# Inner chunks in pairs with row-paired products, and token products spread over a turn, in a vision layer on one core

## The reference

```
h = patches(x) @ W + b                                   # 768 -> 192
h = h + attention(layernorm(h))                          # 12 heads of 16, rope, causal,
                                                         # weights erf(score / 4) + 1, divided by their sum
f = layernorm(h)
shared = silu(f @ s1) * (f @ s3) @ s2                    # 192 -> 768 -> 192, every token
top2 of softmax(f @ Wr) over 8 experts, at most 3920 tokens an expert, by weight
routed[e] = silu(f_e @ w1[e]) * (f_e @ w3[e]) @ w2[e]    # times the token's weight, added to its row
out = h + shared + routed
```

## Time and profile before

| | us |
|---|---|
| median of 3 runs | 3695.66 (3693.1 to 3698.46) |
| profiled execution | 3705.55 |
| its span, first to last instruction | 3703.7 |
| attention stage, about | 0 to 1755 |
| routing stage, about | 1755 to 1909 |
| shared units, about | 1913 to 2378 |
| last shared unit and start of the routed ones | 2378 to 2405 |
| routed units, about | 2405 to 3685 |

### The profile page before, as it was taken

How to read it: one execution, slowest core, us unless ns; L and a number is a source line. 1 busy time by engine, 2 the same in 40 slices (tenths; PEclk the granted TensorE clock), 3 DMA queues, 4 the chain that set the end, 5 groups by cost and what they waited for, 6 DMA issues and landing times. The chain is left out here.

```text
span 3703.7 us, 76882 instructions
## 1 busy us (share of the span) xinstructions
PE 3398.9 (92%) x26932; PEld 2416.6 (65%) x26932; DVE 2472.7 (67%) x4826; ACT 1570.9 (42%) x3198; POOL 1432.8 (39%) x1302
## 2 busy tenths in 40 slices
PE   5999999999999999998249999899999999999997
PEld 4777777777777777776226566666666666666665
DVE  5988898888888989897645555554454444445443
ACT  2444444444444445443014444344444444444443
POOL 0222232222222222232215553136556555555664
PEclk8787788877877888775569999999999999999999
DMA  3332333223323332222012222213232232323222
GB/s 95 71 69 61 75 82 69 68 70 80 69 62 75 82 69 73 65 53 56 35 50 63 66 72 71 83 31 66 38 61 42 59 63 39 60 38 61 41 40 31
DMA packets 330541, 227.05 MB, mean 61 GB/s; under 512 B 209103, under 2 KB 309551, under 8 KB 326159
## 3 DMA queue, kind: packets, MB, share of 16 engines
q1 hardware_dynamic: 259536, 163.94, 17.4%
q0 software_dynamic: 57472, 48.46, 8.8%
q10 hardware_dynamic: 13262, 10.65, 0.8%
HBM read 107.75 MB, written 67.85 MB: 47 GB/s over the span
## 5 line engine op out<-in xcount | busy, mean ns | idle before, releaser
L1272 DVE SCALAR_TENSOR_TENSOR ffn_hidden<-ffn_up,ffn_silu 128x490 f32<-128x490 f32 (+2 forms) x534 | 358.1, 672 | 802.3 <-ACT ffn_silu L1255 731.4
L699 POOL TENSOR_TENSOR weights<-weights,x_pair 128x400 f32<-128x400 f32 x384 | 397.2, 1034 | 918.1 <-DVE weights L563 733.7
L1255 ACT ACTIVATE ffn_silu<-ffn_gate 128x490 f32<-128x490 f32 (+2 forms) x534 | 310.9, 583 | 702.4 <-PE ffn_up L1223 635.7
L615 DVE RECIPROCAL recip<-x_product 128x200 f32<-128x200 f32 x384 | 534.4, 1392 | 0.0
L1240 PE MATMUL ffn_out<-ffn_w_hi,ffn_hidden_hi 128*126 128x192 f16 (+2 forms) x2124 | 522.5, 246 | 0.0
L1242 PE MATMUL ffn_out<-ffn_w_hi,ffn_hidden_lo 128*126 128x192 f16 (+2 forms) x2124 | 522.4, 246 | 0.0
L1241 PE MATMUL ffn_out<-ffn_w_lo,ffn_hidden_hi 128*126 128x192 f16 (+2 forms) x2124 | 522.3, 246 | 0.0
L1428 POOL DMA_INDIRECT out_rows<-done,kept x256 | 425.9, 1664 | 150.4 <-issue 98.1
L1418 POOL DMA_INDIRECT tokens<-dram_x,ids x256 | 279.6, 1092 | 397.5 <-issue 258.9
L750 PE MATMUL bank<-w_qkv,normed_t 96*128 96x192 f32 (+1 forms) x1024 | 399.8, 555 | 19.1 <-ACT normed_t L413 19.1
L1265 DVE TENSOR_TENSOR ffn_hidden_lo<-ffn_hidden,ffn_hidden_hi 128x490 f16<-128x490 f32 (+2 forms) x534 | 355.4, 666 | 8.4
(11 more groups left out here) (181 smaller groups left out, 7429.8 us busy)
## 6 DMA issues: line engine op xcount, KB each, us to landing
patches<-in_patches SPq DMA_DIRECT2D x32, 1176.0 KB, 5.1
ffn_raw<-in_w SPq DMA_DIRECT2D x18, 768.0 KB
dram_x_t<-x_t SPq DMA_DIRECT2D x32, 392.0 KB, 3.1
x_t<-dram_x_t SPq DMA_DIRECT2D x24, 512.0 KB, 5.2
base<-dram_h SPq DMA_DIRECT2D x24, 384.0 KB
out_rows<-sums ACTq DMA_DIRECT2D x24, 384.0 KB
v_held<-v SPq DMA_DIRECT2D x64, 102.0 KB, 2.3
dram_h<-h SPq DMA_DIRECT2D x32, 192.0 KB
```

Of the source, the lines that this page charges most:

```text
L615: nc.vector.reciprocal(recip[:, n % 2], x_product[:, n % 2]).then_inc(inverted, 1)
L699: nc.gpsimd.tensor_tensor(weights[:, n % 4], weights[:, n % 4], x_pair[:, n % 4, ::-1], ALU.mult)\
L1255: nc.scalar.activation(T.silu[:, m % 2, 0:n], T.gate[m % 2][:, 0:n], ACT.Silu, scale=1.0 / (TOKEN_SCALE * WEIGHT_SCALE)).then_inc(T.silued, 1)
L1272: nc.vector.scalar_tensor_tensor(T.hidden[:, m % 2, 0:n], T.up[m % 2][:, 0:n], HIDDEN_SCALE / (TOKEN_SCALE * WEIGHT_SCALE), T.silu[:, m % ...
```

## The change

Two things are done. In the attention stage the token product of images u+2 stands at steps 0, 1, 7 and 8 of a turn, a tile at each, instead of 7, 8 and twice 11; the positions of the bank tuples shift with it, and ACT copies the halves at steps 1 and 8 instead of 8 and 11. In the feed-forward stage the inner chunks are made two at a time. The "lo x far" product takes 64 rows of the array instead of 128: gate's in rows 0 to 63, up's in rows 64 to 127 against a second copy of the far tokens' hi part (`far_again`), both at the end of a pair of chunks. After each pair of chunks comes a third of `tensor_out`, the transposes come after the first pair, and the split of the next unit's tokens moves on ACT and DVE to chunk m = 3, into a second set of buffers. ACT gets one more activation a unit. The clearing of the low weight halves goes away, since all 128 rows are now computed.

```diff
 LN1T, QK, VV, YT, PROJ, X2T, ROUTE, TOK = (
-    (0, 1), (2, 3, 4, 5), (6, 9), (7, 8), (10, 11), (13, 14), (16,), (12, 15))
+    (1, 2), (3, 4, 5, 6), (7, 10), (8, 9), (11, 12), (14, 15), (17,), (0, 13))
...
-                    if n in (8, 11) and has_tokens:
-                        k = n // 11
+                    if n in (1, 8) and has_tokens:
+                        k = n // 8
...
-                    if n in (7, 8) and has_tokens:
-                        if n == 7:
+                    if n in (0, 1, 7, 8) and has_tokens:
+                        if n == 0:
...
-                        tokens(n - 7)
+                        tokens(n if n < 2 else n - 5)
...
-                    if n == 11 and has_tokens:
-                        tokens(2)
-                        tokens(3)
...
-            for w_lo in T.w_lo:
-                for lo in w_lo[0:2]:
-                    n += 1
-                    nc.gpsimd.memset(lo[D - 128:128, INNER:2 * INNER], 0.0).then_inc(enlarged, 1)
-                    pool.wait_ge(enlarged, n)
...
+def tokens_hi(nc, T, slot, near, far, n):
+
+    nc.scalar.activation(T.near_hi[slot][:, 0:n], near, ACT.Copy, scale=TOKEN_SCALE).then_inc(T.tokens_hi, 1)
+
+    nc.scalar.activation(T.far_again[slot][D - 128:128, 0:n], far[D - 128:128], ACT.Copy, scale=TOKEN_SCALE)
+    nc.scalar.activation(T.far[slot][:, 0:n], far, ACT.Copy, scale=TOKEN_SCALE).then_inc(T.tokens_hi, 1)
...
-            nc.tensor.matmul(out, hi[:, far], far_both, start=False, stop=False)
-            last = nc.tensor.matmul(out, lo[:, far], far_both, start=False, stop=True)
-        last.then_inc(T.gated, 1)
+            nc.tensor.matmul(out, hi[:, beyond], far, start=False, stop=False)
+    for m in (2 * pair, 2 * pair + 1):
+        beyond = slice(INNER + m * 128, INNER + (m + 1) * 128)
+        nc.tensor.matmul(T.gate[m % 2][:, 0:n], T.w_lo[ws][0][top, beyond], far[top], start=False, stop=True)\
+          .then_inc(T.gated, 1)
+        nc.tensor.matmul(T.up[m % 2][:, 0:n], T.w_lo[ws][1][low, beyond], far_again[low], start=False, stop=True)\
+          .then_inc(T.gated, 1)
...
+def tensor_out(nc, pe, T, g, slot, ws, tiles, third):
...
+    share = len(tiles) * MI // 3
+    for k in range(third * share, (third + 1) * share):
+        t, m = divmod(k, MI)
...
         if m:
             hi(m - 1)
+        if m == 3:
+            split()
     hi(MI - 1)
...
-                tensor_unit(nc, pe, T, g, ws, XU)
-                if not closing(e, i, 7):
-                    turn(v + 1, half + i % 2, 1 - i % 2)
-                if opening(e, i):
-                    tensor_out(nc, pe, T, g - 1, 0, 0, SHORT)
-                else:
-                    tensor_out(nc, pe, T, g - 1, i % 2, 1 - ws if i == 0 else ws, ROUTED)
+                for part in range(3):
+                    tensor_pair(nc, pe, T, g, 1 - i % 2, ws, XU, part)
+                    if part == 0 and not closing(e, i, 7):
+                        turn(v + 1, half + i % 2, 1 - i % 2)
+                    if opening(e, i):
+                        tensor_out(nc, pe, T, g - 1, 0, 0, SHORT, part)
+                    else:
+                        tensor_out(nc, pe, T, g - 1, i % 2, 1 - ws if i == 0 else ws, ROUTED, part)
```

136 lines of the change are left out of this document (71 added, 65 removed).

## The result

The changed kernel takes **3724.1 us** (median of 4 runs, 3722.0 to 3728.7) against 3694.4 us for the kernel before (4 runs, 3690.7 to 3698.5): ratio 1.0073, 95% interval 1.0049 to 1.0096. It is slower, and lies outside the forecast range of 3560 to 3690.

The account below looks back on a forecast made before the run. It took DVE's work plus PE's low clock to bound attention, and PE, with POOL close behind, the routed units. Terms -91 - 16 - 3 + 19 + 6 + 1 = -84 gave 3621.5 profiled, 3612 us median; range 3560 to 3690.

Parts of the forecast that it names:

- What bounds the kernel, attention: Attention turns: DVE's list is the floor, 47.3 us; the 49.0 and 56.0 us turns differ by PE's clock.
- The attention part: Attention: moving token tiles from step 11 lets step 3's q/k products run at full clock; turns 49.4 us, -91 us.
- rival A: Attention: the clock stays low at step 3, turns 51.5 us, attention gives only -30, total 3672 us; chance 0.16.
- That costs little, because PE waits there for DVE's masks anyway: Attention, step 0: the token tile starts at half clock, 4.3 us instead of 2.15, at little cost.
- Half products: Feed-forward: 64-row halves run at once; a pair of chunks takes 3.92 us instead of 4.13, 0.62 less a routed unit.
- Rival D: Feed-forward: the halves don't run at once, 267 pairs lose 0.2 us each, total 3680 us; chance 0.05.
- Shared units: Feed-forward, 24 shared units: each gets 0.65 us shorter, -16 us.
- Routed units: 64 routed units: gathered rows due 8.5 us earlier, no unit shorter than 19.6 us; -3 us (-38 to +38).
- B's sign: Routed units: no wait for gathered rows before L217 and units of 19.0 us; chance 0.12.
- C: Routed units: gathered rows become the bound, slower; the likelier case, with attention at -30, is 3727 us; chance 0.11.
- Units i = 1: Routed units i = 1: put waits behind ACT's weights, DVE's lower weights hold the second pair; +19 us (0 to +40).
- Last shared unit: Last shared unit: transposes of gathered rows stand behind the first pair, so everything waits for them; 31.9 us against 25.9, +6.

Follow-up runs that it names:

- e14: e12 with token tiles 0 and 1 both at step 2 instead of steps 1 and 2; ratio 0.9515 to the kernel before, attention 1515.0 us.
- e5: The kernel before with PE's attention loop written out, so no jumps back; ratio 0.9882, attention 1607.1 us.
- e6: The changed kernel with PE's attention loop written out; ratio 0.9828 to the kernel before, attention 1613.6 us.
- e8: e6 with token tiles 0 and 1 at steps 1 and 2 instead of 0 and 1; ratio 0.9677, attention 1547.8 us.
- e1: The kernel before with only the attention part of the change; ratio 1.0052, attention 1687.5 us.
- e2: The changed kernel with the attention part taken back, only the feed-forward part left; ratio 0.9986.
- e10: e8 with the transposes behind the second pair of chunks, in the last shared unit behind the third; ratio 0.9636, routed units 1281.0 us.
- e11: e10 with ACT's put ahead of the next expert's upper weights in unit 1 of an expert; ratio 0.9681, routed units 1294.3 us.
- e13: e12 with put ahead of the upper weights and DVE's lower weights at the end of unit 6 instead of unit 1; ratio 0.9559, routed units 1251.2 us.
- e12: e10 with PE's feed-forward loops written out as well; ratio 0.9639, routed units 1267.7 us.

## Why the prediction was wrong

- **What bounds the kernel, attention.** Half right. DVE's list is the floor: 47.3 us were worked out, and 47.8 is what `e14` reached. But "what differs is PE's clock" was read from two rows with different clocks and different lengths, and the long turn of the two was also the one with the loop's jump. The view of waits has the 35.1 us of PE for issue, 13 times, and the prediction reads only DVE's waits in it. Without the jumps (`e5`) the stage of the kernel before is 53 us shorter, the tiles where they were, and its long turn 53.4 us instead of 56 to 57: about half of the alternation was the jump, the other half is gone only in `e14`.
- **The attention part, the step that failed:** "the stretch of small products ahead of step 3 is now broken by two token tiles. If the q/k products of step 3 then run at full clock". They do not, and this is where the forecast gain went. The tiles end two steps of scores and outputs ahead of the transposes of step 3, and that is enough for the clock to fall: 26 of 31 blocks stayed slow. The condition was named with its "if", and the rows had a counterexample that the prediction itself tells (rival A: three small steps after the tile of step 8 the clock was low in step 11). Rival A should have had more than 0.16. With the tile at step 2 the mechanism gives its gain: -66 us from one step's move (`e6` to `e8`), -99 with both tiles there (`e6` to `e14`).
- **The term that was missing.** The move takes the longest block of wide products, 4.3 to 5.9 us, from just ahead of the jump. Of a step that is moved the prediction asked what it does where it arrives, and not what it covered where it stood. The waits at the jumps grew by 42 us, but the stage did not pay all of it: writing the loop out gave 62 us in the changed kernel and 53 in the kernel before, so 9 us more, or 27 if `e1` and `e2` are taken for the two kernels with the loop. What is left of the move without any jump is +6.5 us, where rival A has -30 for turns of 51.5: rival A's condition came true and its gain did not, since the idle time taken from DVE at step 11 came back at steps 1, 3 and 4 (the waits `h_new`, `den` and `by_cos` above).
- **"That costs little, because PE waits there for DVE's masks anyway"** (the tiles of steps 0 and 1 at half clock). Without jumps it is right: DVE is idle for 0.4 us there in `e6`. In the turns with a jump it is idle for 4 to 6 us at the two steps, where the tiles stand right behind the stall. How much of that is the stall and how much the tile, no run separates.
- **Half products.** Right in kind: both halves start at once, a change of form costs 0.09 to 0.13. A pair of chunks takes 3.97 us, not 3.92, so 0.49 us a routed unit instead of 0.62. Rival D is out: gate's and up's half start in the same 10 ns.
- **Shared units.** Forecast -16, which is what the units' length gives (18.23 instead of 18.89 us); measured -23. The rest, up to -55 between other pairs of executions, is units that wait less, perhaps by what was touched in passing ("leaves ACT and DVE more room") and not costed.
- **Routed units.** "PE's 0.62 us turns into a wait of PE for gathered rows" is what happened in kind: 35.1 us in 36 units. `e10` shows it from the other side: with the rows due 5.9 us later all of it is gone. The bound "a unit cannot be shorter than 19.6 us, whatever PE does" holds for the average (19.7 in the positions other than 3, 4 and 8), not for each unit: a third of them took 19.1, and of the waits 18 are of 0.3 to 0.5 us and 10 of over 1.5, where 0.5 to 0.7 in most was forecast. B's sign, no such wait and units of 19.0, did not come. That the total (3724) lies beside C's 3727 is luck: C has +77 us from the last shared unit on and -30 in attention; measured were +35 and +5.
- **Units i = 1.** The size was right, +19 against +21 (positions 3 and 4 of an expert, by eight), the cause only in part. `put` behind the upper weights was named first; moving it ahead made the unit longer (`e11`), and what holds it most is DVE's lower weights (`e13`). Both were run with the transposes behind the second pair, not in the changed kernel itself.
- **Last shared unit.** +6 forecast, +7.3 measured, for the reason given. *End:* +1 forecast, nothing seen.

## What to carry over

When a block of long instructions is moved, read two places: what it does to the clock and to the waiting engines where it arrives, and which wait it covered where it stood, a loop's jump above all. A lower clock is not an explanation of a turn's length until the waits by kind have been read for the same turn. In this kernel PE's clock fell somewhere in every turn shown here; what paid was a wide block directly ahead of the product that others wait for, so that the fall came where PE was ahead.

## What the hardware showed

- **A jump back costs PE its instructions.** In a loop of two turns, 443 products each, PE waited for its issue 2.7 us a jump in the kernel before and 6.0 in the changed one, and each of the jumps has its packets in the `instruction` queue; with its consequences a jump cost the stage 4 to 8 us (the columns of the table above, over 13). At the two jumps of the experts' loop PE waited 5.0 and 4.9 us. At the jumps of the shared units' loop, 264 products a pass, no such wait stands in the trace: 21 of 24 units are 18.23 us long. Straight code of the same length was fetched without a wait (`e12`). The Trainium skill says (Runtime: NRT & Kernel Launch, Instruction fetch mechanics) that a taken branch whose target is outside the part of the program that the engine holds forces a fetch before it can go on; the trace agrees, for long loops pay and the short one doesn't. How much the engine holds no run here shows.
- **The clock falls while PE is busy.** In the attention stage PE shows no gap between the tile of step 1 and the transposes of step 3, and the clock has fallen to its lower level 0.1 us before these. Behind scores and products of 17 and 34 columns it fell in most turns; in the block of 24 products of 192 columns of `e14` it rose, and it stayed up through the q/k products of 384 columns in 30 of 31.
- **Two orders of the same work differ by 99 us.** In the attention stage `e6` and `e14` have the same instructions on every engine; one token tile stands two steps later, one a single step. DVE's idle time falls by 3.1 us a turn, from 4.9 to 1.8, and that times 31 turns is the difference.
